# The third shared group's raw weights load into q and k halves that are no longer read, the turns of step fourteen go first, and the second gate and up product comes in two parts

## The reference

```python
x = L0_attn_x
xn = _layernorm(x)
x = x + attn(xn) + ffn(xn)
# attn: rmsnorm, q/k/v = h @ ternary(qkv_w).T, 16 heads of 32, chunks of 128 tokens:
#   o = scale * (masked(q k^T) v + decayed(q) S);  S <- decay * S + k^T v   (a scan over 16 chunks)
#   two rmsnorms of o, then o @ ternary(proj_w).T
# ffn: shared = (silu(x Wg) * (x Wu)) @ Wd, inner width 1024
#   routed = top 2 of 8 experts, each (silu(x Wg) * (x Wu)) @ Wd with inner width 256
```

## Time and profile before

| | |
|---|---|
| median of 3 runs | 1250.89 us (1250.77 to 1256.94) |
| the profiled execution's own time | 1251.17 us |
| its span on the core | 1249.4 us |
| TensorE busy | 1198.6 us, 96% of the span |
| VectorE, ScalarE, GpSimd busy | 662.2, 476.7 and 491.7 us |
| mean DMA rate | 174 GB/s |

### The profile page before, as it was taken

The page is one execution under the profiler, slowest core; times in us unless marked ns, Lnnn a source line. Parts: engine busy times, 40 slices in busy tenths (PEclk is TensorE's granted clock), DMA queues, the critical chain, the costliest instruction groups (busy, mean ns, idle before and its releaser), DMA issues.

```text
span 1249.4 us, 29233 instructions
## 1 busy us (share of the span) xinstructions
PE 1198.6 (96%) x10768; PEld 812.9 (65%) x10768; DVE 662.2 (53%) x1410; ACT 476.7 (38%) x1031; POOL 491.7 (39%) x432
## 2 busy tenths in 40 slices
PE   3899999999999869999999999999999999999998
PEld 3676677677767647777777544444444577777775
DVE  7888789898989778633333322222222233333333
ACT  6455555556555552322222233333333321111111
POOL 3356656665676300344410322222221044444443
PEclk9999999999999989999999999999999999999999
DMA  8598888788879584344332998877977344444443
GB/s 287 137 235 217 199 221 246 196 224 234 230 203 214 168 246 141 80 109 108 100 114 20 206 231 193 193 192 185 197 196 171 94 156 151 151 152 151 149 153 108
DMA packets 269372, 217.39 MB, mean 174 GB/s; under 512 B 196784, under 2 KB 203056, under 8 KB 269296
## 3 DMA queue, kind: packets, MB, share of 16 engines
q1 hardware_dynamic: 255344, 180.03, 54.3%
q0 software_dynamic: 12848, 35.47, 10.4%
q10 hardware_dynamic: 1104, 0.81, 0.2%
HBM read 115.97 MB, written 56.51 MB: 138 GB/s over the span
## 4 chain that ended last, share of the span: by engine, by line
PE 61%; DMA 1%; DVE 1%; ACT 0%; issue 0%; SPq 0%; DVEq 0%
PE sc L597 26%; PE yp L1620 20%; PE sc L1613 14%; DMA raw<-raw 1%; PE rp L2166 1%; PE rat L2166 1%; DVE work L2016 0%; DVE x1s L1996 0%; ACT work L1850 0%; DVE work L1985 0%; DVE x1s L1994 0%; ACT work L1853 0%; DVE work L2021 0%; DVEq L1543 0%; SPq L1606 0%
## 5 line engine op out<-in xcount | busy, mean ns | idle before, releaser
L597 PE MATMUL sc<-x,WG 128*128 128x256 f16 x3072 | 346.1, 273 | 0.0
L597 PEld LDWEIGHTS sc<-x,WG 128*128 128x128 f16 x3072 | 300.6, 98 | 48.5 <-issue 0.6
L1620 PE MATMUL yp<-WD,work 128*128 128x512 f16 (+1 forms) x1194 | 282.6, 382 | 7.6 <-PEq L638 6.6
L1620 PEld LDWEIGHTS yp<-WD,work 128*128 128x128 f16 x1194 | 116.0, 98 | 139.3 <-issue 33.1
L2016 DVE SCALAR_TENSOR_TENSOR work<-sc,up_inv,work 128x512 f32<-128x512 f32 x63 | 47.3, 751 | 250.2 <-ACT work L1850 250.0
L1597 POOL DMA_INDIRECT raw<-xs_dram,slots x71 | 67.1, 946 | 257.6 <-DMA raw<-raw 125.0
L1850 ACT ACTIVATE work<-sc,gate_inv 128x512 f32<-128x512 f32 x63 | 43.3, 687 | 313.1 <-PE sc L597 313.1
L1613 PE MATMUL sc<-WG,raw 128*128 x564 | 136.8, 379 | 0.4 <-DMA raw<-raw 0.4
L866 PE MATMUL ring<-WG 128*128 128x256 f16 x1024 | 121.1, 275 | 2.0 <-PEq L264 2.0
L2090 POOL DMA_INDIRECT raw<-y_dram,gidx x64 | 62.7, 980 | 145.6 <-DVE gidx L2005 84.1
L866 PEld LDWEIGHTS ring<-WG 128*128 128x128 f16 x1024 | 98.6, 99 | 16.7 <-issue 5.1
(11 more groups left out here) (265 smaller groups left out, 1618.5 us busy)
## 6 DMA issues: line engine op xcount, KB each, us to landing
y_dram<-raw SPq DMA_DIRECT2D x71, 256.0 KB
WD<-in_L_attn_x SPq DMA_DIRECT2D x16, 512.0 KB, 4.4
work<-in_L_ffn_w_gate_up SPq DMA_DIRECT2D x16, 512.0 KB, 4.8
xs_dram<-WG SPq DMA_DIRECT2D x16, 512.0 KB, 3.6
xT_dram<-x SPq DMA_DIRECT2D x16, 512.0 KB, 2.7
WG<-in_L_attn_x SPq DMA_DIRECT2D x16, 512.0 KB, 5.4
x_dram<-WG SPq DMA_DIRECT2D x32, 256.0 KB, 2.2
x<-xT_dram SPq DMA_DIRECT2D x16, 512.0 KB, 7.5
```

The costliest lines, as they stand in the source:

```text
L597: ins = pe.matmul(gu[:, h, f * 2 * P:(f + 1) * 2 * P].rearrange("p (u t) -> p u t", u=2), w[:, kk, b, part * P:(part + 1) * P], x[:, :, a ...
L1620: ins = pe.matmul(y[:], act_hl[a][:, f, :], w[:, f, b, :] if len(w.shape) == 4 else w[:, 0, f, b, :], start=(first and f == 0 and (a, b) = ...
```

## The change

The low and high halves of group 2 are now made from `third`, six views of 128 x 512 in the even halves of kT, qT and qlam, in place of `raw[:, 0]`. Five DMAs bring it in, issued in step 15 before the turns of y, after a wait that holds since step 14's last `o_back`. In step 14 the turns of y are issued ahead of group 0 and x16. In step 15 group 3 is loaded as before, once group 1 is split. TensorE's `gate_up` of group 1 has its first half (the gate columns) ahead of `proj` of sequence 1 and its second half behind it. ScalarE makes two pieces of group 2 ahead of the roots, one between silu and `ah`, three behind it; VectorE makes one before `al`, two before the residual of sequence 1, three behind it. The last hunk is the count for the first routed expert's load, which follows from group 2's raw weights no longer passing through `raw[:, 0]`.

```diff
+        idle = [t[:, 0].rearrange("p g t -> p (g t)").rearrange("p (i c) -> p i c", c=DIM) for t in (kT, qT, qlam)]
+        third = [part[:, i] for part in idle for i in range(2)]
...
+        third_in = sem(c, "third_in")
@@ sync
+            def load_third():
+                sp.wait_ge(S["o_full"], 2 * NCH - 2)
+                for i in range(KT // 2):
+                    for h in range(2):
+                        sp.dma_start(idle[i][:, :, h * FFN:(h + 1) * FFN], k["sgu"][2, h][:, 2 * i:2 * i + 2]
+                                     ).then_inc(third_in, 16)
+                sp.dma_start(idle[2], k["sdn"][2]).then_inc(third_in, 16)
...
                 if norm:
                     sp.wait_ge(S["wmax_ready"], n + 1)
                     load_weights(q + 1, par)
-                elif front:
+                sp.wait_ge(S["x1_ready"], 2 * n)
+                load_xr(q, par)
+                if not front:
+                    load_third()
+                for u in range(B):
+                    turn_y(u, q, par)
+                if front and not norm:
                     sp.wait_ge(S["hl_ready"], 2 * NCH)
                     load_group(sp, k, 0)
                     sp.wait_ge(S["logits_ready"], NCH - 1)
                     sp.wait_ge(xT_out[0], 16 * (NCH // 2))
                     sp.dma_start(x16[:, 0], xT_dram[0]).then_inc(x_ins[0][0], 16)
-                sp.wait_ge(S["x1_ready"], 2 * n)
-                load_xr(q, par)
-                for u in range(B):
-                    turn_y(u, q, par)
                 if not front:
-                    for g in range(2, GROUPS):
-                        sp.wait_ge(split, PIECES * (g - 1))
-                        load_group(sp, k, g)
+                    sp.wait_ge(split, PIECES * 2)
+                    load_group(sp, k, 3)
@@ tensor
                     project("v1", *nxt, st)
                     if not norm:
                         spread_maxima()
+                else:
+                    pe.wait_ge(split, PIECES + KT)
+                    gate_up(pe, sc[:, 2:4], x16[:, 0], WG[:, 1], (0, 1))
                 proj(1, q, par, st)
             run_steps(pe, prologue, step)
-            pe.wait_ge(split, PIECES + KT)
-            gate_up(pe, sc[:, 2:4], x16[:, 0], WG[:, 1]).then_inc(gu_fulls[0], 1)
+            gate_up(pe, sc[:, 2:4], x16[:, 0], WG[:, 1], (2, 3)).then_inc(gu_fulls[0], 1)
@@ scalar
-                act.wait_ge(raw_in[g % 2], 48 * (g // 2 + 1))
+                act.wait_ge(*((third_in, 80) if g == 2 else (raw_in[g % 2], 48 * (g // 2 + 1))))
...
-                    act.activation(dst, raw[:, g % 2, i], ACT.Copy, ...
+                    act.activation(dst, third[i] if g == 2 else raw[:, g % 2, i], ACT.Copy, ...
...
                 high_group(1, range(4, PIECES))
+                high_group(2, range(0, 2))
                 on_root(0, q, par)
                 on_root(1, q, par)
...
-                high_group(2, range(0, 2))
+                high_group(2, range(2, 3))
                 act.wait_ge(UNIT["act_ready"][0], 1)
                 act.activation(ah[:, 0], actv[:, 0], ACT.Copy).then_inc(UNIT["ah_ready"][0], 1)
-                high_group(2, range(2, PIECES))
+                high_group(2, range(3, PIECES))
                 high_group(3, range(PIECES))
@@ vector
-                    v.scalar_tensor_tensor(out=w[:, 1, :], in0=raw[:, g % 2, i], scalar=s_, in1=w[:, 0, :],
+                    v.scalar_tensor_tensor(out=w[:, 1, :], in0=third[i] if g == 2 else raw[:, g % 2, i], scalar=s_, in1=w[:, 0, :],
...
                 residual(0, q, par, st)
+                low_group(2, range(0, 1))
                 v.wait_ge(UNIT["ah_ready"][0], 1)
                 v.tensor_tensor(al[:, 0], actv[:, 0], ah[:, 0], ALU.subtract).then_inc(UNIT["al_ready"][0], 1)
+                low_group(2, range(1, 3))
                 residual(1, q, par, st)
-                low_group(2, range(PIECES))
+                low_group(2, range(3, PIECES))
@@ experts, scalar
-                        act.wait_ge(raw_in[par], 48 * (q + 1 + GROUPS // 2))
+                        act.wait_ge(raw_in[par], 48 * (q + GROUPS // 2 + par))
```

More of the change, by code:

```diff
@@ L1092, in high_group @@
             def high_group(g, some):
-                act.wait_ge(raw_in[g % 2], 48 * (g // 2 + 1))
+                act.wait_ge(*((third_in, 80) if g == 2 else (raw_in[g % 2], 48 * (g // 2 + 1))))
                 for i in some:
                     dst = WG[:, g, i, 0, :] if i < KT else WD[:, g, i - KT, 0, :]
-                    act.activation(dst, raw[:, g % 2, i], ACT.Copy, scale=wscale[:, 2:3] if i < KT else wscale[:, 3:4]
+                    act.activation(dst, third[i] if g == 2 else raw[:, g % 2, i], ACT.Copy, scale=wscale[:, 2:3] if i < KT else wscale[:, 3:4]
                                    ).then_inc(high, 1)
```

## The result

| | before | changed |
|---|---|---|
| median (runs) | 1250.80 us (20) | 1247.66 us (20) |
| range of the runs | 1243.21 to 1256.94 | 1242.62 to 1251.88 |
| profiled execution, span | 1251.17, 1249.4 us | 1251.88, 1250.2 us |

What follows compares the result with a forecast made beforehand. ScalarE, held back by group 2's load, was taken to set the L638 meeting that starts the second block. Starting it 4.8 us earlier plus 0.3 from the clock made 5.1: 1250.9 - 5.1 = 1245.8 us, range 1242.8 to 1249.3.

Steps and rivals of the forecast that it cites:

- Turns first: Step 14: with the queue empty the first turn lands near 414.2, so TensorE's 1.81 us wait goes.
- Group 0's landing: Head of step 15: issued at 414.6, landing at 422.3, between 421.4 and 423.4; step 15 gains 0.6 us.
- past 424: Head of step 15: a split of group 0 later than 424 would prove the prediction wrong.
- C: Rival, loads late: group 0 at 423.4, group 3 taking 8.9 us; gain 1.0, 1249.9 us; chance 0.14.
- Rival D: Slower: group 0's late landing delays step 15; gain used up at 427.1, 1253.5 us at 430; chance 0.04.
- A lowered clock in step 15: Head of step 15: no term for it; TensorE was to be ready at 424.9, ScalarE at 426.1.
- From group 1 split to the second block: End of step 15: group 1 split at 440.6, second block at 451.9, which is 4.8 us before 456.71.
- The third load: Step 15: five DMAs from 423 to 426, in by 435, cost nothing; ScalarE's 4.81 us wait for group 2 goes.
- the wait of 1.5: End of step 15: ScalarE waits 1.45 us for group 3, landing at 447.8, ahead of its last six pieces.
- the 450: End of step 15: group 3 consumed after 450 would prove the prediction wrong.
- The second product in parts: Step 15: fills TensorE's 2.32 us ahead of the second `proj`; worth nothing by itself, as ScalarE ends later.
- The clock at L638: Falls in a 4.8 us gap too, costing 1.7 to 2.8: gain 0.3, bounds none or 2.4.

Runs made afterwards that it cites:

- e6: Changed kernel plus 16 idle matmuls ahead of step 15's first `o_back`, filling TensorE's gap; stretch 48.04 us, ratio 0.9964.
- e10: Changed kernel with x16's load moved from directly behind group 0 to behind step 14's last store; stretch 48.30 us, ratio 0.9982.
- e5: Changed kernel with the second gate and up product whole again, behind `proj` of the second sequence; stretch 47.83 us, ratio 0.9958.
- e9: Changed kernel with group 0 loaded ahead of the residual's x and the turns, x16 behind them, second product whole; stretch 44.94 us, ratio 0.9937.
- r1: Changed kernel run again unaltered, on another chip; stretch 49.69 us, ratio 0.9975.
- e1: Changed kernel with step 14's old queue order, group 0 and x16 ahead of the residual's x and the turns; stretch 46.13 us, ratio 0.9959.
- e2: Kernel before with only step 14's turns put first, nothing else changed; stretch 54.28 us, ratio 1.0023.
- e3: Changed kernel with group 0's load ahead of the residual's x and the turns, only x16 behind them; stretch 44.24 us, ratio 0.9955.
- e7: e3 plus 18 idle matmuls behind TensorE's last product, ahead of L638; stretch 45.80 us, ratio 0.9937.
- e8: Changed kernel in which SP waits for step 14's second turn to land before issuing group 0; stretch 49.81 us, ratio 0.9972.
- e4: Changed kernel with group 0's load at the head of step 14, ahead of the turns of x; stretch 49.86 us, ratio 0.9974.

## Why the prediction was right, and where it was off

By its own steps, in the two profiled executions. To put a time of the changed kernel on the scale of the prediction, 1.96 us are taken off.

- **Turns first:** 1.81 us forecast; `proj` came 1.87 earlier. Right.
- **Group 0's landing:** issued at 414.6 as forecast (416.60 less 1.96). The landing was forecast at 422.3, 7.7 us behind the first issue, with 8.8 as the far bound. The group was consumed 10.05 behind it (416.60 to 426.65), at 424.7 on the prediction's scale: past 424, which it had named as a sign of being wrong. This is the step that failed. The forecast lay below both groups that had been measured (8.5 and 8.8), for no reason but a shorter queue behind; and the far bound left out the slowest third DMA, though C used it for group 3: 416.5 + 8.9 = 425.4 would have covered the landing, and the third DMA did take 8.8. SP's issue of 4.06 us is seen beside it, but e6 shows the same landing without it on the group's own DMAs. `take_oT` was to start 0.6 us earlier and started 1.64 later (22.37 against 20.73 us behind the second `o_back`). Rival D had the mechanism, and put the landing that uses up the gain at 12.5 us; the truth lay between C's 8.8 and that.
- **A lowered clock in step 15:** not foreseen. I had said that TensorE is ready 1.2 us ahead of ScalarE there; with the true landing the gap is 4.26 us and takes the clock. Group 1's last low piece ended 3.2 us later than before (446.34 - 407.97 = 38.37 against 441.18 - 406.01 = 35.17): 1.64 by the load, and the other 1.6 behind it, where the clock was low. With the gap filled (e6) the stretch is 1.6 shorter. But the cost differs with the moment at which the clock rises: e10, with the gap unfilled, was only 0.3 above e6.
- **From group 1 split to the second block:** forecast 451.9 - 440.6 = 11.3 us; measured 457.64 - 446.34 = 11.30, before 15.53. The third load, the freed ScalarE, the 6.2 us of group 3's third DMA (447.34 to 453.54) and the wait of 1.5 all came as worked out. This is where the gain comes from. (On the prediction's scale group 3 was consumed at 451.6, past the 450 that it had named as a sign of being wrong, but only because step 15 ran late as a whole.) The Trainium skill's fit of 2.0 us plus bytes over 436 GB/s, made for the GpSimd path ("DMA: Bandwidth & Descriptors", section on the anatomy of one DMA), gave an estimated 5.6 us for a group. This group took 7.2 from its first issue (446.37 to 453.54), so the measurement decides for the rows.
- **The second product in parts:** forecast to be worth nothing in the stretch, and e5, with the product whole, was not longer. It empties TensorE ahead of L638, with a gap of 4.79 us against 0.47 (e5) and 2.19 (e9) with the product whole. In e5 the clock was full at `down`, but it had just fallen and risen; in e9 it fell at L638 all the same. So that the parts cost the clock there is not shown.
- **The clock at L638:** it fell, as forecast, with 0.3 us of gain and bounds 0 and 2.4; the clock's stretch gave 1.34 in these two. The eight traces with a like gap gave 0.2 to 1.5 against the one trace of before, so a good part of the 1.34 may be chance. The Trainium skill, "TensorE: Matmul & The Clock Gate", section on oscillation in real kernels, describes waits between bursts of matmuls that bring the clock back down, and counts the loss as half the time spent at half rate. The traces agree: the `down` of before took 5.28 us where 12 such matmuls take 2.75.

Sum of the traces: +3.2 - 4.23 = -1.03 for the stretch, where 4.8 of gain were forecast, and -1.34 for the clock: 2.4 against 5.1. The median's 3.1 is a little more than the traces show; how much of step 15 runs at half clock differs between kernels with the same gap in step 15 (stretches from 47.8 to 49.7 in e5, e10 and r1). That the result fell into the range is in part luck: the range reached into C, whose two late loads are not what happened. Group 0 was later than C had it (10.05 us against 8.8), group 3 landed as forecast (6.2 against C's 8.9), and the low clock in step 15 had no term at all. A small slip of reading: the two bubbles of the middle in the earlier trace rows are the 14th and 15th digits, which are slices 13 and 14 only when counted from 0.

## What to carry to other kernels

When a load is moved behind other DMAs of one queue, don't price it below the landings that were measured, and let the bound reach to the slowest of them: here the group took 10.05 us where the rows had 8.5 and 8.8. A late load costs twice if it leaves the matmul engine idle: here the clock fell in the gap of 4.26 us and the next matmuls ran slow. And of two reorderings packed into one change, measure each alone: here one was worth 4.6 us in the stretch (e1 against before) and hid that the other cost 3.6 (e2 against before), while loading group 0 first and only x16 behind the turns (e3, e7, e9) took 4.9 to 6.5 us off the stretch, against 1.0 in the changed kernel.

## What the runs showed of the hardware that I had not expected

- A DMA of 512 KB issued as the third behind two DMA transposes held SP's queue for 3.97 to 4.06 us in five traces (changed, r1, e2, e5, e10). In e6 that third took 0.51 and the fourth, x16, 3.37. When the first was issued only after the transposes had landed, the third took 0.50 (e8). Behind the two transposes of step 15 no issue took over 1.63 us (before). The cause is open.
- The clock was lost in a gap of only 2.19 us of TensorE at L638 (e9), and in one of 2.83 in step 14 (e4); it held in a gap of 0.72 at L638 (e7) and in gaps of 1.73 and 2.32 in step 15 (before).
- Two DMA transposes (the turns of x) issued right behind a group's three loads landed 7.9 to 8.2 us after their issue (e4); the same two took 3.3 to 4.7 before.
- TensorE waited 1.81 and 1.37 us for step 14's first turn with 2.6 MB ahead of it on the queue (before, e1), and 0, 0.39 and 1.34 us with 2.1 MB (e3, e9, e7).
